# Two attention pipelines on one core: where TensorE waits before the scores, how wide the first score matmul is, and which engine squares the clamped scores

## The reference, cut to what matters

```python
neg_inner = jnp.einsum('bhie,bhje->bhij', tq, tk) - jnp.einsum('bhid,bhjd->bhij', sq, sk)
dist = jnp.arccosh(jnp.maximum(neg_inner, 1.0 + 1e-07))
scores = -dist ** 2 / np.sqrt(D)
scores = jnp.where(causal[None, None], scores, -jnp.inf)
attn = jax.nn.softmax(scores, axis=-1) * spike_mask
```

## Time and profile before

| | |
|---|---|
| median of 3 runs | 2266.14 us (2264.39 to 2266.26) |
| profiled execution, its own time | 2264.88 us |
| its span, first to last instruction | 2263.1 us |
| hyper pipeline in it | about 1262 to 1407 us |
| rope pipeline in it | about 1873 to 1990 us |

### The profile page before, as it was taken

How to read it: one execution, slowest core, us unless ns; L and a number is a source line. 1 busy time by engine, 2 the same in 40 slices (tenths; PEclk the granted TensorE clock), 3 DMA queues, 4 the chain that set the end, 5 groups by cost and what they waited for, 6 DMA issues and landing times. The chain is left out here.

```text
span 2263.1 us, 32388 instructions
## 1 busy us (share of the span) xinstructions
PE 2072.3 (92%) x11764; PEld 1736.5 (77%) x11764; DVE 1118.8 (49%) x1969; ACT 941.4 (42%) x1879; POOL 665.8 (29%) x713
## 2 busy tenths in 40 slices
PE   7999999999999999999998776899899667867998
PEld 6888888888888888888886555688799355747998
DVE  3333443444344434434445785333577655756775
ACT  4242323324242332324224697222355453454664
POOL 3030201203030110303000496120387152308884
PEclk9999999999999999999999698899999788978999
DMA  4010010101000010200002101310255132146661
GB/s 160 1 56 1 7 50 0 56 0 56 0 37 19 0 56 0 81 0 0 1 1 54 42 35 62 112 44 3 83 198 165 38 66 96 68 137 206 212 216 57
DMA packets 93436, 139.98 MB, mean 62 GB/s; under 512 B 15438, under 2 KB 70384, under 8 KB 93360
## 3 DMA queue, kind: packets, MB, share of 16 engines
q1 hardware_dynamic: 86304, 122.97, 17.1%
q0 software_dynamic: 4928, 12.86, 1.6%
q10 hardware_dynamic: 2128, 3.15, 0.4%
HBM read 106.96 MB, written 12.06 MB: 53 GB/s over the span
## 5 line engine op out<-in xcount | busy, mean ns | idle before, releaser
L584 DVE TENSOR_TENSOR cond_h<-cond_silu,ps 128x512 f32<-128x512 f32 x288 | 197.8, 687 | 696.9 <-ACT cond_silu L495 693.4
L495 ACT ACTIVATE cond_silu<-ps 128x512 f32<-128x512 f32 x288 | 172.3, 598 | 771.8 <-PE ps L414 771.8
L414 PE MATMUL ps<-a_x_hi,cond_w_hi 128*128 128x512 f32 x1152 | 449.5, 390 | 2.0 <-DVE a_x_lo L262 2.0
L414 PE MATMUL ps<-a_x_lo,cond_w_hi 128*128 128x512 f32 x1152 | 448.9, 390 | 0.0
L414 PE MATMUL ps<-a_x_hi,cond_w_lo 128*128 128x512 f32 x1152 | 448.9, 390 | 0.0
L383 POOL TENSOR_TENSOR cond_w_lo<-cond_stage_up,cond_w_hi 128x256 fp32r<-128x256 f32 x144 | 108.5, 772 | 832.8 <-ACT cond_w_hi L476 832.8
L414 PEld LDWEIGHTS ps<-a_x_hi,cond_w_hi 128*128 128x128 f32 x1152 | 216.8, 188 | 47.4 <-DVE a_x_lo L262 2.4
L414 PEld LDWEIGHTS ps<-a_x_lo,cond_w_hi 128*128 128x128 f32 x1152 | 216.8, 188 | 44.9
L414 PEld LDWEIGHTS ps<-a_x_hi,cond_w_lo 128*128 128x128 f32 x1152 | 216.6, 188 | 45.1
L430 PE MATMUL ps<-cond_h_hi,cond_d_hi 128*128 128x512 f32 x576 | 224.4, 390 | 3.4 <-DVE cond_h_lo L552 3.4
L430 PE MATMUL ps<-cond_h_hi,cond_d_lo 128*128 128x512 f32 x576 | 224.1, 389 | 0.0
(11 more groups left out here) (371 smaller groups left out, 4117.6 us busy)
## 6 DMA issues: line engine op xcount, KB each, us to landing
moe_stage_up<-in_L_ffn_expert_wv SPq DMA_DIRECT2D x22, 1024.0 KB, 8.3
typed_stage_up<-in_L_cond_wi SPq DMA_DIRECT2D x11, 1024.0 KB, 4.9
typed_stage_dn<-in_L_cond_wo SPq DMA_DIRECT2D x11, 1024.0 KB
moe_stage_dn<-in_L_ffn_expert_proj SPq DMA_DIRECT2D x11, 1024.0 KB
cond_stage_up<-in_L_cond_Wg SPq DMA_DIRECT2D x7, 1024.0 KB, 4.8
cond_stage_up<-in_L_cond_Wu SPq DMA_DIRECT2D x7, 1024.0 KB, 6.8
cond_stage_dn<-in_L_cond_Wd SPq DMA_DIRECT2D x7, 1024.0 KB, 5.0
hyp_v_now<-hyp_v_blk SPq DMA_DIRECT2D x16, 272.0 KB, 2.3
```

What stands on the lines that cost most here:

```text
L414: ins = pe.matmul(up_ps[st % 2][j], w[:, j, k, fs], x[:, k, tok], start=(i == 0), stop=(i == 3 * KC - 1))
L495: act.activation(silu[:, st % 2], up_ps[st % 2][0], ACT.Silu).then_inc(act_done, 1)
L584: dve.tensor_tensor(h[:, st % 2], silu[:, st % 2], up_ps[st % 2][1], ALU.mult).then_inc(up_free, 1)
```

## The change

In the hyper attention the square leaves ScalarE. VectorE computes it in a new phase `square` as max(s, 1 + 1e-7) times z, in one fused instruction that reads the scores in PSUM and z in SBUF. The phase stands directly behind `clamp` in VectorE's list, with the same lag (1) and the same two conditions as before: the clamp of its pair, and `wait(dve, masked, i - 1)`. The semaphore `clamped`, for which TensorE's next scores and ScalarE's `root_log` wait, is now given by the square.

In both attentions the first score matmul now has 64 columns like the others. In the hardware loop the three waits of `score` (q taken, k blocked, the score banks free) are moved to the instruction in front of it: the last transpose of `y_turn` in hyper, the last matmul of `mix` in rope. In the written-out iterations they stay with `score`.

```diff
-            lag = dict(turn=0, q_blk=0, k_blk=0, score=0, clamp=1, root_sq=1, root_ln=2, root=2, root_add=2, dist_ln=2,
+            lag = dict(turn=0, q_blk=0, k_blk=0, score=0, clamp=1, square=1, root_ln=2, root=2, root_add=2, dist_ln=2,
                        dist=3, mask=3, top=3, shift=3, prob=4, p_turn=4, p_take=4, mix=5, y=5, y_turn=5, y_take=6,
                        out=6, add=6, stretch=0, fetch=3)
             order = dict(tensor="mix out turn p_turn y_turn score",
-                         scalar="y_take dist root_ln prob root q_blk root_sq p_take dist_ln",
-                         vector="stretch clamp y add k_blk top", gpsimd="mask root_add shift", sync="fetch")
+                         scalar="y_take dist root_ln prob root q_blk p_take dist_ln",
+                         vector="stretch clamp square y add k_blk top", gpsimd="mask root_add shift", sync="fetch")
...
-                    def score(i, q, nth):
+                    def score_ready(i):
+
                         pe.wait_ge(q_taken, i + 1)
                         pe.wait_ge(k_blocked, i + 1)
                         wait(pe, clamped if hyper else masked, i)
+
+                    def score(i, q, nth):
+
+                        if isinstance(i, int):
+                            score_ready(i)
                         for n in range(8):
                             c, j, r = n // 4, n // 2 % 2, n % 2
-
-                            seq, feat, h = slice(0 if n == 0 else j * T, (j + 1) * T if n else P), slice(r * T, (r + 1) * T), (r * KC + c) * GH
+                            seq, feat, h = slice(j * T, (j + 1) * T), slice(r * T, (r + 1) * T), (r * KC + c) * GH
...
+                                if not hyper and not isinstance(i, int) and (hp, j) == (HP - 1, 1):
+                                    score_ready(i + lag["mix"] - lag["score"])
                                 ins = pe.matmul(y_ps[j * T:(j + 1) * T, hp * 2 * VW:(hp + 1) * 2 * VW],
...
                         for c in range(KC):
+                            if hyper and not isinstance(i, int) and c == KC - 1:
+                                score_ready(i + lag["y_turn"] - lag["score"])
                             ins = pe.transpose(yT_ps[:, c * P:(c + 1) * P], y[:, q, c * P:(c + 1) * P], m.ident)
...
-                    def root_square(i, q, nth):
-                        act.wait_ge(clamped, i + 1)
-                        wait(act, masked, i - 1)
-                        act.activation(t[:, q], z[:, q], ACT.Square).then_inc(root_squared, 1)
-
                     def root_log(i, q, nth):
-                        act.wait_ge(root_squared, i + 1)
+                        act.wait_ge(clamped, i + 1)
...
-                            dve.tensor_scalar(z[:, q], s_ps, float(np.float32(1.0 + 1e-7)), None, ALU.max).then_inc(clamped, 1)
+                            dve.tensor_scalar(z[:, q], s_ps, float(np.float32(1.0 + 1e-7)), None, ALU.max).then_inc(bounded, 1)
...
+                    def square(i, q, nth):
+
+                        dve.wait_ge(bounded, i + 1)
+                        wait(dve, masked, i - 1)
+                        dve.scalar_tensor_tensor(t[:, q], s_ps, float(np.float32(1.0 + 1e-7)), z[:, q], ALU.max, ALU.mult).then_inc(clamped, 1)
```

More of the change, by code:

```diff
@@ L1000, in attention @@
             sem(n) for n in ("stretched", "turned", "k_turned", "q_taken", "k_blocked"))
-        scored, clamped, root_squared, root_logged, rooted = (
-            sem(n) for n in ("scored", "clamped", "root_squared", "root_logged", "rooted"))
+        scored, bounded, clamped, root_logged, rooted = (
+            sem(n) for n in ("scored", "bounded", "clamped", "root_logged", "rooted"))
         root_added, dist_logged, dist_done, masked = sem("root_added"), sem("dist_logged"), sem("dist_done"), sem("masked")
@@ L1141, in take_q, with root_log @@
                         act.activation(qT[:, q].rearrange("p c n -> p (c n)"), qT_ps, ACT.Copy).then_inc(q_taken, 1)
-                    def root_square(i, q, nth):
+                    def root_log(i, q, nth):
                         act.wait_ge(clamped, i + 1)
-                        wait(act, masked, i - 1)
-                        act.activation(t[:, q], z[:, q], ACT.Square).then_inc(root_squared, 1)
-                    def root_log(i, q, nth):
-                        act.wait_ge(root_squared, i + 1)
                         act.activation(t[:, q], t[:, q], ACT.Ln, bias=m.minus_one[:]).then_inc(root_logged, 1)
@@ L1179, in y_take @@
                         act.activation(yT[:, q].rearrange("p c n -> p (c n)"), yT_ps, ACT.Copy).then_inc(y_taken, 1)
-                    run(act, "scalar", dict(q_blk=take_q, root_sq=root_square, root_ln=root_log, root=root, dist_ln=dist_log, dist=dist, prob=exponential, p_take=p_take, y_take=y_take))
+                    run(act, "scalar", dict(q_blk=take_q, root_ln=root_log, root=root, dist_ln=dist_log, dist=dist, prob=exponential, p_take=p_take, y_take=y_take))
                 @block.vector
@@ L1240, in add @@
                         ins.then_inc(added, 1)
-                    run(dve, "vector", dict(stretch=stretch, k_blk=block_k, clamp=clamp, top=top, y=scale_y, add=add))
+                    run(dve, "vector", dict(stretch=stretch, k_blk=block_k, clamp=clamp, square=square, top=top, y=scale_y, add=add))
                 @block.gpsimd
```

## The result

The changed kernel takes 2277.38 us (median of 5 runs, 2276.47 to 2279.48), the kernel before 2265.11 us (5 runs). The ratio is 1.005 with a 95% interval of 1.0036 to 1.0064: slower by 12.3 us (8 to 14.5 by the interval). The prediction was 2281 us, slower by 15.

A forecast was written before the change was run, and what follows sets the result against it. No single engine's work bounded either pipeline; a repeating chain of steps did, 7.67 us a lap in hyper, 5.94 in rope. Hyper's +22.5 and rope's -7.2 gave +15.3, forecast as 2281 us, range 2273 to 2291.

The forecast's parts named there:

- ScalarE's square at nothing: Hyper: removing ScalarE's 16 squares of 1.05 us saves nothing, since POOL's root_add (2.35 us) covers them.
- The square's duration: Hyper: the fused square on VectorE takes 1.22 us, like the rope clamp.
- its new ring: Hyper: mask, square, reciprocal, y, add, k_blk, top, shift, next mask form a repeating chain of 9.62 us against 7.67.
- The sum of hyper: Hyper pipeline: +22.5 us in all, of which +23.0 from the longer laps.
- 13 laps: Hyper: squares of pairs 2 to 15 wait for masks 0 to 13; these laps take 121.9 us against 99.0.
- VectorE waits again behind the clamp: Hyper: stretch and clamp take 0.68 to 2.20 plus 1.14 us behind top, shift and mask 4.7, so VectorE waits.
- The narrow matmul: First score matmul with 64 columns: all 16 score passes take 1.09 us in place of 1.69, 0.60 less.
- four rounds: Scores: matmuls fall on four quarters of TensorE's array, so 14 and 16 passes, by fours, both need four rounds.
- The moved wait: Rope's loop: the last mix matmul now runs after k_blk, costing 0.30 us an iteration (bounds 0.06 to 0.36).
- Rope's sum: Rope: 2 cold iterations x 1.1, 4 written-out x 0.5 and 10 loop x 0.30 make 7.2 us less.
- +15.3: Whole kernel: +22.5 us from hyper and -7.2 from rope make it 15.3 us slower.
- one term of 1.1 us: Hyper's filling: the first narrow scores save about 1.1 us.

The follow-up runs named there:

- the square ahead of top: The changed kernel with the square moved from behind the clamp to directly ahead of top in VectorE's list: 2257.39 us, ratio 0.9952 against the kernel before.
- TensorE kept busy in hyper: The changed kernel with the square behind top, plus eight unused matmuls in hyper's loop ahead of the last y_turn transpose: 2264.87 us.
- the two parts: Changed kernel with only the square moved to VectorE, scores as before: 2292.43 us; kernel before with only the score changes of both attentions: 2255.60 us.

## Why the prediction was right

**ScalarE's square at nothing: right.** In the square ahead of top most of its time turned into ScalarE's wait, 0.35 to 1.21 us, at the same lap.

**The square's duration and its new ring: right.** Predicted 1.22 us and a lap of 9.62; measured 1.22 and 9.61. Every link was in the rows of before, among them the 0.08 us from top to shift, which came from rope. That it fits to 0.01 is luck: the mask's end releases the square after 0.10 us, not 0.03, and shift takes 2.25 to the next start, not 2.32. That the place and not the instruction costs the time is shown by moving the phase alone: 2277 to 2257 us.

**The sum of hyper: right.** Predicted +22.5 us for the pipeline, of which +23.0 in 13 laps; measured +21.75 from the first stretch to the end of the last add, of which +22.95 in the 13 laps, -1.0 ahead of the first mask and -0.25 in the last two laps. Single laps were less exact and balanced: the first took 9.14 us where the sum has 8.31, the thirteenth 9.23 where it has 9.62, and some between were 0.1 shorter.

**VectorE waits again behind the clamp: right,** with 2.2 to 3.1 us before the square.

**The narrow matmul: right in mechanism and in size.** Predicted 1.09 us with four rounds, measured 1.09; at the low clock 2.0 was worked out and 1.98 measured.

**The moved wait: right in sign, mis-sized.** I took 0.30 us from half of the two wide passes' 0.60; it measures 0.24 alone, and from the end of k_blk to the scores 0.31 in place of 0.11, so 0.20 in the changed kernel. A loop iteration gave 0.37 us in place of 0.30. The 0.30 held a change of the array's shape, for which I had no row; no run separates it from the two passes and the waits, and all together cost less than I took.

**Rope's sum: short.** Predicted -7.2 us. The clamps' span alone gave 7.2, the first scores, ahead of it, 1.1, and the drain another 1.1 (from the last clamp to the start of the last mix 8.89 us before, 7.81 after). There p_turn and out of one pair took 1.97 and 1.60 us before and 1.10 and 1.06 after: they no longer ran at the low clock. I had not counted the drain. It is 7.8 us in every kernel with the narrow scores in rope but one (9.0 with TensorE kept busy in hyper), and 8.7 to 8.9 in the three with the wide ones. Together it is -9.6 between the end of hyper and the end of rope's last mix.

**Where the 3 us between +15.3 and +12.3 are.** The two profiled executions differ by 12.2 us. Rope gave 2.4 more than forecast, and hyper cost 0.75 less. The rest cancels: the changed kernel's hyper pipeline began 0.7 us later, though nothing ahead of it was changed, and what lies behind the pipelines was 0.65 shorter, both of no known cause.

**What the forecast did not hold** is additivity. By the traces of the two parts the narrow scores are worth some 4 us in hyper's filling and last laps when the square is on VectorE, where I had only one term of 1.1 us, and the 3.3 us by which the totals fail to add up are in line with it.

## What to carry to other kernels

A wait keeps its meaning when its instruction moves, but not its price: before moving work to an engine that has time to spare, look which iteration the awaited step belongs to and when in that iteration it ends, and list what is queued behind the moved instruction. Where the awaiting phase stood late in its engine's list, put it late in the new one, here directly ahead of the step that waits for the same event; that was 20 us between two lists with the same instructions. And take off the path only what is on it: ScalarE was the busiest engine of this pipeline, and its square lay wholly inside a POOL instruction.

## What the runs showed that was not expected

Here TensorE did more in less time when it was kept busy: eight unused matmuls per iteration raised the granted clock from 0.81 to 0.96 over 80 us, and the kernel went from 2268.57 to 2264.87 us. Where a ring passes through TensorE, its idle gaps can cost twice, as waiting and as mix and out at 1.93 and 2.08 us in place of 1.13 and 1.16. The kernel before had them at 1.92 and 2.08 us too, at 1381 and at 1389 us, and its laps stayed at 7.60 to 7.67: there the clamp released the scores, and TensorE was not in the ring. With the square on VectorE it is the square that releases them.

A matmul with 64 rows and 128 weight columns ahead of seven with 64 columns costs 0.60 of 1.69 us. In the kernel before its two passes take 0.67 us, and the other 14 begin 0.60 us after these began, at 1921.72, so next to nothing runs beside the two:

```profile
1921.12 0.67 PE L1093 MATMUL ps<-rope_k_blk,rope_qT 64*128 64x256 f32 x2 [0.51 <-issue]
```

The same matmul with 64 columns adds nothing to the 1.09 us of the others.
